# Transition matrices with time outermost, gathered per group by ScalarE, norms compacted by TensorE, and scales made between the query operations

## The chip, the cores and the metric

The kernel runs on one core of one Trainium2 chip. The metric is the device time of one launch in microseconds. 2335.91 us is the median of three runs of the kernel before (2333.31 to 2340.91).

## The reference

The layer is a recurrent mixer followed by a feed-forward block, on 8 rows of 512 time steps. Only the mixer is touched. For every head, with states `z` and `s` of N = 32 by DH = 16, it steps through time:

```
bc = (value @ W_bc.T).reshape(B, T, H, 4, N)
bc = bc / (sqrt(sum(bc*bc, axis=-1)) + EPS)          # Bz, Bx, Cz, Cx
S = 1 / (1 + dt*k + dt*dt*A)
z = S * (z - dt*A*s + dt*(Bz * u))
s = s + dt*z + dt*(Bx * u)
y = Cz . z + Cx . s
```

There are H = 32 heads. The scalars `dt` and `k` are of one head and time step, `A` is of one head and state.

## The kernel before

The program has three blocks: `project`, `mix` and `ffn`. `mix` works on 64 units, one for each row b (8) and group of four heads (8). A unit's 128 partitions are 4 heads by 32 states. Time is cut into NC = 8 chunks of C = 64 steps, all chunks computed in parallel, and only the states at the ends of chunks are passed on in order.

Each engine runs its own stream of instructions over the units, with semaphores between them. A loop over b runs seven times, its body unrolled over the 8 groups, and an eighth copy of the body stands behind it.

*TensorE* (`product`, `sum_squares`, `transpose_k`, `inner`, `outputs`): in a unit it transposes `k` (L716), makes three quarters of a product for the unit two ahead (L670), the states of the chunks `dX` (L704), the rest of that product, the scores (L695), two more products, in `outputs` a fourth one, the even inner outputs (L743), the sums of squares `ps_s` of the unit two ahead (L682: one matmul of 512 columns for each of the four vectors Bz, Bx, Cz, Cx), the outer outputs (L755) and the odd inner outputs (L743). Then it waits for the next `k`.

*ScalarE*: squares and copies each product (`evacuate`, L818 and L819), takes the root of the sums into `rows` (`norms`, L827), copies `kT`, `dX` and `y`, multiplies one row of the shear by A (`scale_beta`, L808), and makes the determinant `det` by a logarithm and an exponential (L858, L864).

*VectorE*: `body` scales the four vectors by the inverse norms (L1036, L1040), makes `k` (L1046 to L1060) and the queries `q` (L1065 to L1076), then `end` and `coef`, the scales of the next unit (`scales`: add epsilon, invert, multiply by the factors), the chain of states over the chunks (`V`, `cross`, `X`: L1098, L1103, L1109, seven times), the masked scores `g` (L1115) and a running sum for `det` (`log_sum`, L983). Between these, `advance(1)` puts one operation of `step_psi`: the 2 by 2 transition matrix of each chunk, `psi`, is stepped through its 64 time steps, for half of the groups (HALF = 4) at a time, four units ahead at least. A step is two operations on 128 partitions by 128 elements: `prod = psi * shear` (L958) and `psi = psi + prod` (L962), each waiting for the one before it. With 128 operations for a half and four units for it, 32 stand in a unit. `psi` is laid out as [row, component, group, chunk, time] and `shear` as [component, group, time], so time is the innermost axis and an operation of one time step takes every 65th element of `psi` and every 64th of `shear`.

*SyncE* issues the loads: the shear (`load_n_alpha`, `load_beta`), the norms' rows as a compact tile (`compact_norms`, four transfers for each unit between ScalarE's root and VectorE's scales), the scales to DRAM and back, spread over the partitions (`spread_scales`).

At the start, before the loop, the first half of row 0 is stepped alone (`step_rows`, L972 and L976, 256 operations of 128x64), with the first unit's scales in the middle.

## Time and profile before

| | |
|---|---|
| median of three runs | 2335.91 us |
| the profiled execution's own time | 2331.21 us |
| its span, first to last instruction | 2329.6 us |
| `mix` loop, unit 0 of row 0 to unit 0 of row 7 | 306.79 to 1812.81 us |
| VectorE busy, 1000 to 1500 us | 477.93 of 500 us |
| TensorE busy, 1000 to 1500 us | 428.09 of 500 us |
| ScalarE busy, 1000 to 1500 us | 238.69 of 500 us |
| granted TensorE clock, 1000 to 1500 us | 0.95 |

An engine is busy while one of its instructions runs. Matmuls overlap, and their ends are modelled. The granted clock is the share of full speed.

### The profile page before, as it was taken

What the parts mean: (1) busy time and instruction counts of PE and PEld (TensorE: products, weight loads), DVE (VectorE), ACT (ScalarE), POOL (GpSimd) and SP (SyncE); (2) the same over time, 40 slices, a digit from 0 to 9 for tenths busy, and PEclk for the clock granted to TensorE, in tenths of its full rate; (3) what the DMA queues carried; (4) which work ended last, traced back from release to release, by engine and by line L of the source; (5) the groups of instructions that cost most, each with busy time, mean ns of one, the idle gap of its engine ahead of it and who ended that gap; (6) DMA issues with size and microseconds to landing.
All of it is one profiled execution on the core that took longest, in us unless ns stands there. A gap on an engine that the chain in (4) does not pass through costs nothing. (4 is left out here: it accounts for less than half of the span.)

```text
span 2329.6 us, 78341 instructions
## 1 busy us (share of the span) xinstructions
PE 1875.7 (81%) x31266; PEld 1078.5 (46%) x31266; DVE 2050.5 (88%) x5467; ACT 1083.9 (47%) x1700; POOL 84.5 (4%) x28
## 2 busy tenths in 40 slices
PE   6777468987888898888888889887888898367886
PEld 3333134444444444444444444444444444246775
DVE  6887599999999999999989989998999998487774
ACT  4665235454444454445544444544545455034553
POOL 0000000000000000000000000000000000153300
PEclk9898779999999999999999999999999999578997
DMA  4555634655555565545655554665455543433400
GB/s 139 178 214 184 178 92 112 147 134 131 124 127 125 119 150 130 125 106 134 145 123 126 138 124 109 145 143 125 110 126 129 117 113 87 159 154 136 145 27 27
DMA packets 224663, 300.25 MB, mean 129 GB/s; under 512 B 96784, under 2 KB 114192, under 8 KB 218128
## 3 DMA queue, kind: packets, MB, share of 16 engines
q1 hardware_dynamic: 174416, 212.11, 35.9%
q10 hardware_dynamic: 48704, 78.68, 13.3%
q8 instruction: 252, 4.13, 0.8%
q0 software_dynamic: 1152, 4.19, 0.5%
q14 instruction: 139, 1.14, 0.2%
HBM read 240.85 MB, written 50.86 MB: 125 GB/s over the span
## 5 line engine op out<-in xcount | busy, mean ns | idle before, releaser
L670 PE MATMUL m_ps_a<-m_valT,m_w_bc 128*128 128x512 f32 x2048 | 962.1, 619 | 59.8 <-DMA m_valT<-scratch_valT 32.0
L670 PEld LDWEIGHTS m_ps_a<-m_valT,m_w_bc 128*128 128x128 f32 x2048 | 389.8, 198 | 491.1 <-issue 483.7
L958 DVE TENSOR_TENSOR m_prod<-m_psi,m_shear 128x128 f32<-128x128 f32 x960 | 369.0, 384 | 0.0
L962 DVE TENSOR_TENSOR m_psi<-m_psi,m_prod 128x128 f32<-128x128 f32 x960 | 368.4, 384 | 0.0
L818 ACT ACTIVATE m_sq<-m_ps_a 128x512 f32<-128x512 f32 x256 | 152.8, 597 | 372.4 <-PE m_ps_a L670 367.9
L833 ACT ACTIVATE m_kT<-m_ps_g 128x512 f32<-128x512 f32 x128 | 72.0, 596 | 249.8 <-PE m_ps_g L716 249.8
L716 PE MATMUL m_ps_g<-m_ident,m_k 128*128 128x128 f32 x512 | 88.9, 330 | 103.8 <-DVE m_k L1060 103.5
L695 PE MATMUL m_ps_g<-m_q,m_k 32*64 32x64 f32 x8192 | 122.8, 232 | 45.3 <-issue 38.9
L695 PEld LDWEIGHTS m_ps_g<-m_q,m_k 32*64 32x64 f32 x8192 | 107.5, 133 | 100.2 <-ACT m_dX L840 53.3
L819 ACT ACTIVATE m_raw<-m_ps_a 128x512 f32<-128x512 f32 x256 | 151.6, 592 | 0.0
L755 PEld LDWEIGHTS m_ps_y<-m_q,m_X 32*16 32x16 f32 x7168 | 105.2, 94 | 84.1 <-issue 84.1
L755 PE MATMUL m_ps_y<-m_q,m_X 32*16 32x64 f32 x7168 | 119.5, 218 | 28.9 <-issue 28.9
L221 PE MATMUL ps_w<-p_xnT,w_in 128*128 128x512 f32 x256 | 118.5, 617 | 14.6 <-ACT gate L284 14.6
L840 ACT ACTIVATE m_dX<-m_ps_g 128x128 f32<-128x128 f32 (+1 forms) x128 | 26.8, 261 | 221.5 <-PE m_ps_g L704 209.3
L716 PEld LDWEIGHTS m_ps_g<-m_ident,m_k 128*128 128x128 f32 x512 | 70.1, 168 | 115.9 <-DVE m_k L1060 113.8
L1036 DVE TENSOR_TENSOR m_raw<-m_raw,m_scale 128x1024 f32<-128x1024 f32 x64 | 77.5, 1210 | 49.7 <-issue 29.5
L743 PE MATMUL m_ps_y<-m_g,m_u 64*16 64x64 f32 x4096 | 89.8, 224 | 32.3 <-issue 25.4
L1267 POOL TENSOR_TENSOR f_y<-f_y,f_gate 128x2048 f32<-128x2048 f32 x8 | 38.4, 4805 | 1975.8 <-DMA f_svg<-scratch_svgT 1878.4
L743 PEld LDWEIGHTS m_ps_y<-m_g,m_u 64*16 64x16 f32 x4096 | 63.4, 95 | 89.5 <-issue 83.2
L827 ACT ACT_TABLE_LOAD x64 | 82.1, 1283 | 43.3 <-PE m_ps_s L682 43.2
L704 PEld LDWEIGHTS m_ps_g<-m_u,m_kT 64*32 64x32 f32 x7168 | 68.0, 106 | 63.9 <-issue 63.7
L1287 PE MATMUL f_ps_o<-f_w_out,f_y 128*128 128x256 f32 x256 | 61.6, 401 | 34.8 <-POOL f_y L1269 34.8
(143 smaller groups left out, 3061.7 us busy)
## 6 DMA issues: line engine op xcount, KB each, us to landing
m_scale<-scratch_norm SPq DMA_DIRECT2D x256, 256.0 KB, 5.3
m_w_bc<-in_w_bcT ACTq DMA_DIRECT2D x252, 256.0 KB, 4.7
m_shear<-scratch_n_alpha SPq DMA_DIRECT2D x64, 256.0 KB, 5.3
m_shear<-scratch_beta SPq DMA_DIRECT2D x256, 64.0 KB, 4.1
m_det<-scratch_gd SPq DMA_DIRECT2D x256, 64.0 KB, 4.5
scratch_gateT<-gate SPq DMA_DIRECT2D x8, 1024.0 KB, 3.9
scratch_valT<-val SPq DMA_DIRECT2D x8, 1024.0 KB, 4.5
scratch_svgT<-svg SPq DMA_DIRECT2D x8, 1024.0 KB, 5.5
```

The costliest lines, as they stand in the source:

```text
L221: mm = pe.matmul(ps_w[i % BANKS].ap(), w_in[:, k, col:col + P], xnT[:, k, :], start=(k == 0), stop=(k == KD - 1))
L670: mm = pe.matmul(ps_a[j % 2].ap(), w_bc[:, j, kt, :], valT[:, kt, :], start=(kt == 0), stop=(kt == KI - 1), skip_group_check=True)
L695: mm = pe.matmul(ps_g[rows_of(c), h, into], k[heads, part, cols], q[s][heads, part, cols], start=(part == 0), stop=(part == 1), skip_group ...
L716: mm = pe.transpose(ps_g[:, part, pair * P:(pair + 1) * P], k[:, part, pair * P:(pair + 1) * P], ident.ap())
L743: mm = pe.matmul(ps_y[h * N:h * N + DH, c * C:(c + 1) * C], u[rows_of(c), s, c // 2, h * DH:(h + 1) * DH], g[rows_of(c), h, c // 2 * C:(c ...
L755: pe.matmul(ps_y[h * N:h * N + DH, cols], X[heads, c - 1, part, :], q[s][heads, part, cols], start=False, stop=(part == 1), skip_group_che ...
L818: act.activation(sq[:, j, :], ps_a[j % 2].ap(), ACT.Square).then_inc(sq_ready.sem, sq_ready.step)
L819: act.activation(raw[s][:, j, :], ps_a[j % 2].ap(), ACT.Copy).then_inc(raw_ready.sem, raw_ready.step)
L827: act.activation(rows_.ap(), ps_s.ap(), ACT.Sqrt).then_inc(norm_ready.sem, norm_ready.step)
L958: dve.tensor_tensor(prod.ap(), psi_t[half][:, :, :, :, t], shear_t[half][:, :, :, t].unsqueeze(1).to_broadcast([P, 2, 2, HALF * NC]), ALU. ...
L962: ins = dve.tensor_tensor(psi_t[half][:, :, :, :, t + 1], psi_t[half][:, :, :, :, t], prod[:, :, ::-1, :], ALU.add)
L1036: dve.tensor_tensor(r4[:, 0:2, :], r4[:, 0:2, :], scale[:, 0:2, :], ALU.mult).then_inc(own.sem, own.one())
```

## The change

`psi` and `shear` get time as the outermost axis, so that the 128 elements of one time step lie together. The four groups of a half lie side by side in them. Since the operations on `k` and `q` need time innermost, ScalarE copies each unit's `psi` (2080 elements in a partition, read with a step of 128 elements) into a tile `psi_g` of the old form (`gather_psi`), and VectorE waits for it ahead of `k`. The shear is loaded into `stage` and laid out by two ScalarE copies with strided output for each group (`lay_shear`), instead of one in place.

`sum_squares` is cut into 8 segments of 64 columns. For each segment and vector a matmul with a selection matrix `seg_sum` puts the sums of head h and segment s into row h*8+s, so that the norms leave as a compact tile of 128x64, by 32 matmuls of 64 columns instead of 4 of 512. The root is taken straight into `compact`; the four transfers of `compact_norms` are gone.

The three operations of the scales stand between the queries' operations. `log_sum` stands ahead of `g`. `kt` uses the memory of `scale`, so SyncE loads the next scales after `q_ready`. The operations of `step_psi` are given to the four units as 36, 36, 36 and 20. At the start the shears of the first four groups are loaded into `raw`, and ScalarE lays them out by eight copies once all are there, before the first step; the gather of the first unit stands ahead of the evacuations of the second. `project` stores `beta` a second time, one more small transfer for each row.

```diff
+    SHARES = (0, 36, 72, 108, 2 * C)
...
-        psi = sb("psi", [P, 2, 2, HG, NC, C + 1])
-        shear = sb("shear", [P, 2, HG, T])
+        psi = sb("psi", [P, 2, C + 1, 2, 2, HALF * NC])
+        psi_g = sb("psi_g", [P, 2, 2, NC, C + 1])
+        shear = sb("shear", [P, 2, C, 2, HALF * NC])
+        stage = sb("stage", [P, 2, T])
         prod = sb("prod", [P, 2, 2, HALF * NC])
...
-        kt = sb("kt", [P, 2, T])
+        kt = scale[:, 0:2, :]
+        kT = sb("kT", [P, 2, T])
...
-                    sp.wait_ge(scaled.sem, scaled.at(b, group - 1))
+                    sp.wait_ge(q_ready.sem, q_ready.at(b, group - 1))
...
-                    for j in range(NJ):
-                        mm = pe.matmul(ps_s[j * N:(j + 1) * N, :], head_sum.ap(), sq[:, j, :],
-                                       start=True, stop=True, skip_group_check=True)
+                    for seg in range(SEGS):
+                        for j in range(NJ):
+                            mm = pe.matmul(ps_s[j * N:(j + 1) * N, 0:SEG], seg_sum[:, seg, :],
+                                           sq[:, j, seg * SEG:(seg + 1) * SEG],
+                                           start=(seg == 0), stop=(seg == SEGS - 1), skip_group_check=True)
...
-                def scale_beta(b, group):
-                    act.wait_ge(beta_in[group].sem, beta_in[group].at(b, HP - 1))
-                    act.activation(shear[:, 0, group, :], shear[:, 0, group, :], ACT.Copy,
-                                                  scale=A[:, group:group + 1]).then_inc(beta_scaled.sem, beta_scaled.step)
+                def lay_shear(b, group, src, loads=None):
+                    cols = slice(group % HALF * NC, (group % HALF + 1) * NC)
+                    dst = [shear[:, group // HALF, :, comp, cols].rearrange("p t c -> p c t") for comp in range(2)]
+                    act.wait_ge(shear_in.sem, shear_in.at(b, (loads or group + 1) * HP - 1))
+                    act.wait_ge(stepped.sem, stepped.at(b - 1, group // HALF))
+                    act.activation(dst[0], chunks(src[:, 0, :]), ACT.Copy, scale=A[:, group:group + 1])
+                    act.activation(dst[1], chunks(src[:, 1, :]), ACT.Copy).then_inc(shear_ready.sem, shear_ready.step)
+                def gather_psi(b, group):
+                    half, cols = group // HALF % 2, slice(group % HALF * NC, (group % HALF + 1) * NC)
+                    act.wait_ge(stepped.sem, stepped.at(b, group // HALF))
+                    act.wait_ge(raw_used.sem, raw_used.at(b, group - 1))
+                    act.wait_ge(coef_ready.sem, coef_ready.at(b, group - 1))
+                    act.activation(psi_g.ap().rearrange("p r k c t -> p (r k) c t"),
+                                   psi[:, half, :, :, :, cols].rearrange("p t r k c -> p (r k) c t"),
+                                   ACT.Copy).then_inc(psi_ready.sem, psi_ready.step)
...
-                    act.wait_ge(compact_in.sem, compact_in.at(b, group * NJ - 1))
-                    act.activation(rows_.ap(), ps_s.ap(), ACT.Sqrt).then_inc(norm_ready.sem, norm_ready.step)
+                    act.wait_ge(rows_stored.sem, rows_stored.at(b, group - 1))
+                    act.activation(compact.ap(), ps_s[:, 0:SEG], ACT.Sqrt).then_inc(norm_ready.sem, norm_ready.step)
...
+                        if more:
+                            gather_psi(b, group + 2)
                         if not last and group < LAST:
-                            scale_beta(b + 1, group + 1)
+                            lay_shear(b + 1, group + 1, stage)
...
-                            dve.tensor_tensor(prod.ap(), psi_t[half][:, :, :, :, t],
-                                              shear_t[half][:, :, :, t].unsqueeze(1).to_broadcast([P, 2, 2, HALF * NC]),
-                                              ALU.mult).then_inc(steps.sem, steps.one())
+                            dve.tensor_tensor(prod.ap().rearrange("p r k c -> p r (k c)"),
+                                              psi[:, half, t].rearrange("p r k c -> p r (k c)"),
+                                              shear[:, half, t].rearrange("p k c -> p (k c)").unsqueeze(1
+                                              ).to_broadcast([P, 2, 2 * HALF * NC]), ALU.mult).then_inc(steps.sem, steps.one())
                         else:
-                            ins = dve.tensor_tensor(psi_t[half][:, :, :, :, t + 1], psi_t[half][:, :, :, :, t],
+                            ins = dve.tensor_tensor(psi[:, half, t + 1], psi[:, half, t],
                                                     prod[:, :, ::-1, :], ALU.add)
...
+                def add_eps(b, group):
+                    dve.wait_ge(norm_ready.sem, norm_ready.at(b, group))
                     dve.tensor_scalar(compact.ap(), compact.ap(), NORM_EPS, None, ALU.add).then_inc(own.sem, own.one())
-                    between(1)
-                    dve.wait_ge(own.sem, own.n)
+                    return own.n
+                def invert_norms(eps_added):
+                    dve.wait_ge(own.sem, eps_added)
                     dve.reciprocal(compact.ap(), compact.ap()).then_inc(own.sem, own.one())
-                    between(1)
+                    return own.n
+                def apply_factors(b, group, inverted):
                     dve.wait_ge(factor_in.sem, factor_in.at(b, 3 * (group + 1) - 1))
-                    dve.wait_ge(own.sem, own.n)
+                    dve.wait_ge(own.sem, inverted)
                     dve.tensor_tensor(compact.ap(), compact.ap(), factor.ap(), ALU.mult).then_inc(rows_ready.sem, rows_ready.step)
...
+                        dve.wait_ge(psi_ready.sem, psi_ready.at(b, group))
...
+                        if here:
+                            eps_added = add_eps(b, group + 1)
+                        dve.tensor_tensor(by_chunk(q[s].ap())[:, ::-1], over_rows_of(r4[:, 3, :]),
+                                          psi_g[:, :, 0, :, 1:], ALU.mult).then_inc(raw_used.sem, raw_used.step)
                         cz_made = own.n
                         advance(1)
...
+                        if here:
+                            inverted = invert_norms(eps_added)
...
+                        if here:
+                            apply_factors(b, group + 1, inverted)
                         dve.tensor_tensor(q[s][:, 1, :], q[s][:, 1, :], kt[:, 0, :], ALU.subtract).then_inc(q_ready.sem, q_ready.step)
...
-                        if not (last and group == LAST):
-                            scales(b, group + 1, advance)
...
+                        if not (last and group == LAST):
+                            log_sum(b, group + 1)
```

TensorE, `outputs` of a unit: the even inner outputs (L743 before, L730 after), then the sums of squares of the unit two ahead. Before:

```order
L743 MATMUL m_ps_y<-m_g,m_u 16x64 [waits m_y_ready]
L743 MATMUL m_ps_y<-m_g,m_u 16x64 x15
L679 REGISTER_ALU
L680 REGISTER_ALU [waits m_sq_ready]
L682 MATMUL m_ps_s<-m_sq,m_head_sum 32x512 [waits m_norm_ready]
L682 MATMUL m_ps_s<-m_sq,m_head_sum 32x512 x3
```

After the change:

```order
L730 MATMUL m_ps_y<-m_g,m_u 16x64 [waits m_y_ready]
L730 MATMUL m_ps_y<-m_g,m_u 16x64 x15
L664 REGISTER_ALU
L665 REGISTER_ALU [waits m_sq_ready]
L668 MATMUL m_ps_s<-m_sq,m_seg_sum 32x64 [waits m_norm_ready]
L668 MATMUL m_ps_s<-m_sq,m_seg_sum 32x64 x31
```

The 4 matmuls of 512 columns are 32 of 64 columns; the profile counts two instructions and two weight loads for each, so 8 become 64. The waits and the neighbours are the same.

VectorE, from the second product of the queries (`m_q` on) towards the chain of states; `m_compact` is the tile of the scales. Before:

```order
L1068 TENSOR_TENSOR m_q<-m_raw,m_psi 128x2x512
L958 TENSOR_TENSOR m_prod<-m_psi,m_shear 128x128 [waits m_steps_dve]
L1074 TENSOR_TENSOR m_q<-m_kt,m_q 128x512 [waits m_raw_used,m_own_dve]
L962 TENSOR_TENSOR m_psi<-m_psi,m_prod 128x4x32 [waits m_steps_dve]
L1076 TENSOR_TENSOR m_q<-m_q,m_kt 128x512
L1080 TENSOR_TENSOR m_end<-m_det,m_e_end 128x16 [waits m_e_end_in]
L958 TENSOR_TENSOR m_prod<-m_psi,m_shear 128x128 [waits m_steps_dve]
L1085 TENSOR_TENSOR m_coef<-m_psi,m_end 128x32 [waits m_own_dve]
L962 TENSOR_TENSOR m_psi<-m_psi,m_prod 128x4x32 [waits m_steps_dve]
L997 ISA
L998 TENSOR_SCALAR m_compact<-m_compact 128x64 [waits m_compact_in]
L958 TENSOR_TENSOR m_prod<-m_psi,m_shear 128x128 [waits m_steps_dve]
```

After the change (`m_scale` is the tile that `kt` shares):

```order
L1076 TENSOR_TENSOR m_scale<-m_raw,m_psi_g 128x1024 [waits m_k_ready,m_own_dve]
L968 TENSOR_TENSOR m_psi<-m_psi,m_prod 128x128 [waits m_steps_dve]
L1002 REGISTER_ALU
L1003 TENSOR_SCALAR m_compact<-m_compact 128x64 [waits m_norm_ready]
L1081 TENSOR_TENSOR m_q<-m_raw,m_psi_g 128x2x512
L963 TENSOR_TENSOR m_prod<-m_psi,m_shear 128x128 [waits m_steps_dve]
L1008 RECIPROCAL m_compact<-m_compact 128x64 [waits m_own_dve]
L1089 TENSOR_TENSOR m_q<-m_scale,m_q 128x512 [waits m_raw_used,m_own_dve]
L968 TENSOR_TENSOR m_psi<-m_psi,m_prod 128x128 [waits m_steps_dve]
L1012 ISA
L1014 TENSOR_TENSOR m_compact<-m_compact,m_factor 128x64 [waits m_own_dve,m_factor_in]
L1093 TENSOR_TENSOR m_q<-m_q,m_scale 128x512
```

The scales' three operations (the first stands last but one in the listing of before, its two followers behind it) move up from behind `coef` to between the queries' operations, and the first waits for ScalarE's root instead of a transfer.

ScalarE, from the logarithm of a unit (`m_det`) to the next evacuation of a product (`m_sq`, `m_raw`). Before:

```order
L858 ACT_TABLE_LOAD
L858 ACTIVATE m_det<-m_det,m_one,m_nA 128x512 [waits m_gd_in1]
L808 ACTIVATE m_shear<-m_shear,m_A 128x512 [waits m_beta_in2]
L816 REGISTER_ALU
L818 ACTIVATE m_sq<-m_ps_a 128x512 [waits m_sums_made,m_a_made]
L819 ACTIVATE m_raw<-m_ps_a 128x512
L821 DMA m_w_bc<-in_w_bcT 128x512
```

After the change:

```order
L859 ACT_TABLE_LOAD
L859 ACTIVATE m_det<-m_det,m_one,m_nA 128x512 [waits m_gd_in1]
L808 ACTIVATE m_psi_g<-m_psi 128x2080 [waits m_coef_ready,m_raw_used,m_stepped]
L797 ISA
L799 ACTIVATE m_shear<-m_stage,m_A 128x8x64 [waits m_stepped,m_shear_in]
L800 ACTIVATE m_shear<-m_stage 128x8x64
L817 REGISTER_ALU
L819 ACTIVATE m_sq<-m_ps_a 128x512 [waits m_sums_made,m_a_made]
L820 ACTIVATE m_raw<-m_ps_a 128x512
L822 DMA m_w_bc<-in_w_bcT 128x512
```

The gather, with three waits, and a second copy for the shear now stand between the logarithm and the evacuation that TensorE's products wait for.

## Rows read from the trace of the kernel before

**Rows 1.** The page: busy time, share of span and instructions of each engine.
```profile
PE 1875.7 (81%) x31266; PEld 1078.5 (46%) x31266; DVE 2050.5 (88%) x5467; ACT 1083.9 (47%) x1700; POOL 84.5 (4%) x28
```

**Rows 2.** Timeline of VectorE, first operation of units: start, duration, [idle before, releaser].
```profile
306.79 1.21 DVE L1036 TENSOR_TENSOR m_raw<-m_raw,m_scale 128x1024 f32<-128x1024 f32 x1
...
1035.52 1.23 DVE L1036 TENSOR_TENSOR m_raw<-m_raw,m_scale 128x1024 f32<-128x1024 f32 x1
...
1061.13 1.20 DVE L1036 TENSOR_TENSOR m_raw<-m_raw,m_scale 128x1024 f32<-128x1024 f32 x1
...
1386.26 1.22 DVE L1036 TENSOR_TENSOR m_raw<-m_raw,m_scale 128x1024 f32<-128x1024 f32 x1 [4.75 <-issue]
...
1812.81 1.22 DVE L1036 TENSOR_TENSOR m_raw<-m_raw,m_scale 128x1024 f32<-128x1024 f32 x1 [1.87 <-DMA m_scale<-scratch_norm]
```

**Rows 3.** Waits of all engines, 300 to 1900 us: us in total, times, longest.
```profile
PE m_ps_g L716 <- DVE m_k L1060: 98.0, 47, 6.7
...
PE m_ps_g L695 <- issue: 35.9, 42, 1.4
...
PE m_ps_y L755 <- issue: 28.9, 16, 3.7
...
PE m_ps_y L743 <- issue: 24.5, 15, 3.2
```

**Rows 4.** Timeline of TensorE in the last row of the batch.
```profile
1948.78 1.09 PE L716 MATMUL m_ps_g<-m_ident,m_k 128*128 128x128 f32 x8
...
1966.79 0.64 PE L743 MATMUL m_ps_y<-m_g,m_u 64*16 64x64 f32 x32
1967.54 1.06 PE L682 MATMUL m_ps_s<-m_sq,m_head_sum 128*32 128x512 f32 x8
1968.54 1.75 PE L755 MATMUL m_ps_y<-m_q,m_X 32*16 32x64 f32 x112
...
1970.79 1.09 PE L716 MATMUL m_ps_g<-m_ident,m_k 128*128 128x128 f32 x8
```

**Rows 5.** Two stretches, the first behind a wait for `k`: us, TensorE busy (instructions), granted clock, DMA share, GB/s.
```profile
1232.00:1238.00 6.00, 5.81 (x27) 0.62 0.10 21
...
1948.00:1970.00 22.00, 21.78 (x477) 1.00 0.36 78
```

**Rows 6.** VectorE by line and shape, 300 to 1900 us: busy, mean ns, idle before.
```profile
L962 DVE TENSOR_TENSOR m_psi<-m_psi,m_prod 128x128 f32<-128x128 f32 x946 | 363.0, 384 | 0.0
L1103 DVE TENSOR_TENSOR m_cross<-m_coef,m_V 128x64 f32<-128x64 f32 x354 | 76.5, 216 | 0.0
...
L1074 DVE TENSOR_TENSOR m_q<-m_kt,m_q 128x512 f32<-128x512 f32 x59 | 40.5, 686 | 0.0
```

**Rows 7.** Timeline of VectorE in the chain of states of one unit.
```profile
1057.00 0.38 DVE L958 TENSOR_TENSOR m_prod<-m_psi,m_shear 128x128 f32<-128x128 f32 x1
1057.30 0.18 DVE L1109 TENSOR_TENSOR m_X<-m_cross 128x32 f32<-128x32 f32 x1
1057.42 0.40 DVE L962 TENSOR_TENSOR m_psi<-m_psi,m_prod 128x128 f32<-128x128 f32 x1
```

**Rows 8.** ScalarE by line and shape, 300 to 1900 us, then 200 to 300 us.
```profile
L808 ACT ACTIVATE m_shear<-m_shear,m_A 128x512 f32<-128x512 f32 x56 | 38.9, 707 | 0.0
L864 ACT ACTIVATE m_det<-m_det 128x512 f32<-128x512 f32 x60 | 37.9, 631 | 30.8 <-DVE m_det L983 30.3
...
L277 ACT ACTIVATE ek<-p_compact 128x128 f32<-128x128 f32 x1 | 0.3, 292 | 0.0
```

**Rows 9.** Timeline of ScalarE behind the logarithm of one unit.
```profile
1272.12 0.60 ACT L818 ACTIVATE m_sq<-m_ps_a 128x512 f32<-128x512 f32 x1 [2.75 <-PE m_ps_a L670]
...
1275.55 0.60 ACT L818 ACTIVATE m_sq<-m_ps_a 128x512 f32<-128x512 f32 x1 [2.35 <-PE m_ps_a L670]
```

**Rows 10.** VectorE by line and shape, 225 to 306 us, where row 0 starts.
```profile
L976 DVE TENSOR_TENSOR m_psi<-m_psi,m_prod 128x64 f32<-128x64 f32 x128 | 28.8, 276 | 0.0
...
L998 DVE TENSOR_SCALAR m_compact<-m_compact 128x64 f32<-128x64 f32 x1 | 0.2, 196 | 6.2 <-DMA m_compact<-m_rows 6.2
```

137 lines of the change are left out of this document (59 added, 78 removed).

## The prediction

> **What bounds the kernel now.** I read the page first: VectorE is busy for 88% of the span, TensorE for 81%, ScalarE for 47% [rows 1]. Then the timeline of VectorE at the first operation of each unit. In the loop a unit with no wait takes 1061.13 - 1035.52 = 25.6 us on VectorE [rows 2], back to back. Seven rows of the batch take 1812.81 - 306.79 = 1506.0 us [rows 2], 215.1 us for each row of 8 units. That is 8 x 25.6 = 204.8 us and 10.3 us of waits; about half of these is the start of a loop turn, where VectorE stands for 4.75 us with nothing that releases it ("issue") [rows 2].
>
> VectorE is the bound, but not by far. TensorE waits for `k` 98.0 us in 1600 us, 59 units, which is 1.7 us a unit [rows 3]. In the last row of the batch no steps are made, so VectorE is light there, and TensorE shows its own length: from one unit's transposes to the next 1970.79 - 1948.78 = 22.0 us [rows 4], with the full work and almost no gap. In ordinary units it also stands inside its bursts of small matmuls, again on "issue": 35.9 + 28.9 + 24.5 = 89.3 us in those 59 units [rows 3], 1.5 us each. So TensorE's own length is 22.0 + 1.5 = 23.5 us against VectorE's 25.6, and what VectorE saves beyond 2.1 us in such a unit is not to be had.
>
> **The steps on VectorE.** The 32 step operations of a unit take 384 ns each at 128x128 [rows 6]. Two neighbours with contiguous operands give the line for contiguous ones: 216 ns at 64 elements and 686 ns at 512 [rows 6], 1.05 ns an element, 283 ns at 128. The difference, 100 ns, is what taking every 64th or 65th element costs, 0.78 ns for each. The chain of dependences doesn't hide it: the operation after a step starts 0.30 us behind it, the next step 0.12 us later, when the first (0.38 us) has just ended [rows 7]; a step of 0.28 us lets both move up by 0.10 us. Bounds: nothing, if the stride isn't the reason, and 0.17 us, if the step came down to the 216 ns of half the elements. I take 0.10, since both operands become contiguous: 32 x 0.10 = 3.2 us, so 22.4 us a unit. In the units with 36 operations four stand in a row at the end, where each waits out the one ahead (0.28 and a few hundredths instead of 0.20): 3 x 4 x 0.12 us in four units, some 0.4 each, so 22.8 us.
>
> The Trainium skill ("SBUF — State Buffer", section "SBUF: two separate sides") says that SBUF is read in lines of 16 bytes and that an access which crosses to a new line each time pays a penalty. The trace agrees, with 384 against 283 ns; the page gives no figure. The same rule speaks against the change on ScalarE, which now does the strided walk.
>
> **The gather and the lays on ScalarE.** No row has ScalarE jump through memory. Contiguous copies from SBUF take 292 ns at 128 and 631 ns at 512 elements [rows 8], 0.88 ns each, so 2080 elements take 2.0 us at least. With VectorE's extra of 0.78 ns on each it is 3.6 us. As the far end I take four times the contiguous price, 7.4 us. I take 3.6, since the walk is of the same kind (a new place for each element). The two lays, 512 elements each with a strided output, are 0.63 + 0.40 = 1.0 us each by the same extra, in place of one of 0.71 [rows 8]. Together 3.6 + 2.0 - 0.7 = 4.9 us more, all of it between the logarithm and the next evacuation. Queued behind it is that evacuation, which frees the buffer of TensorE's fourth product. There ScalarE waits 2.75 us for TensorE now, and at the next product 2.35 us more [rows 9]: TensorE makes that product, 1275.55 - 1272.12 = 3.4 us, in the other buffer before it needs this one, and the evacuation itself takes 3.4 - 2.35 = 1.1, so 2.3 us of delay pass unseen. The room is 2.75 + 2.3 = 5.0 us, and 4.9 just fit. The gather's own waits don't count: `coef` is made on VectorE before the chain of states starts, while ScalarE still copies `dX`; in the two units of eight where the last steps stand in the chain of states, they end in its middle. On the other side, VectorE needs `psi_g` only after the chain of states, `g` and two multiplies of the next unit; its wait there would hold `k` and with it TensorE's transposes.
>
> **The norms on TensorE.** The sums take 1968.54 - 1967.54 = 1.0 us now [rows 4]. After, they are 64 instructions of 64 columns on 32 output rows. The nearest row is the even inner outputs, 32 instructions of 64 columns that go to four column groups in turn as these do: 0.64 us, 20 ns each [rows 4]. 64 x 20 = 1.25 us, 0.25 more. From below: no more than now, since as many columns pass. From above: the transposes, 8 with 128 columns of weights and 128 moving, 1.09 us [rows 4], which is 136 ns each or 0.53 ns a column; 96 columns for each of the 64 would be 51 ns, 3.3 us, 2.3 more.
>
> The Trainium skill ("TensorE: Matmul & The Clock Gate", section "Part 3: Packing small matmuls — row/col tiling") says that a weight load overlaps with running matmuls only when the row group differs; here all four vectors use all rows. By it the dear end would hold. The even inner outputs all stand on the same rows too and go at 20 ns, so the trace speaks against it.
>
> TensorE has to be fed 56 more matmuls and as many weight loads in each unit, 64 x 56 = 3584 beside the program's 31266 [rows 1], all inside a burst. I let the "issue" gaps grow from 1.5 to 1.9 us; bounds are the 1.5 of now and 2.8 (a gap of a microsecond more for the second half of a burst that is twice as long).
>
> **The scales and the transfers.** The removed transfers cost VectorE little in the loop, where nothing but the loop's start and single late scales (1.87 us once [rows 2]) holds up a unit. I cost them at nothing. The root is taken before ScalarE copies `kT`, so the first operation of the scales finds it there. SyncE now waits for the lay of the group ahead before it loads a shear; the scales behind that in its queue are due half a unit later. They are loaded after `q_ready`, under the chain of states (20 pairs as in rows 7, 20 x 0.32 = 6.4 us), `log_sum` and `g`; without that cover they would come late as in rows 2, by 2 us or more. `log_sum` ahead of `g` makes `g` 1.2 us later, covered by the products that TensorE makes between scores and outputs.
>
> **The start.** Before row 0's loop VectorE waits 6.2 us for the compact norms [rows 10]; that goes. The 256 operations of 128x64 at 276 ns [rows 10] come to 216 [rows 6], but every one has a neighbour to overlap, so about 0.04 us each, 10 us in all. Against it: eight lays of 1.0 us, which begin when all loads are there, put off the first step by some 6 us, and the first gather (3.6 us) stands ahead of the second unit's evacuations. Together -6 us.
>
> **The sum.** VectorE 22.8 us, TensorE 22.0 + 0.25 + 1.9 = 24.15 us: TensorE is the bound. As each waits for the other within a unit (`k`, `dX`, the scores), I add 0.15: 24.3 us. The start of a loop turn stays, 5 us. A row is 8 x 24.3 + 5 = 199.4 us, 15.7 less than 215.1. Seven rows: -110. The last row: four units at 24.3, -6, and the rest, bound by TensorE already, +1. The start: -6. Together -121: the profiled execution's own 2331.2 us becomes 2210. The median of the runs is 4.7 us above that execution, so 2215. The granted clock enters through the 22.0 us, a row at the upper level: a stretch behind a wait for `k` shows 0.62, this unit 1.00 [rows 5], and with TensorE as the bound such waits are left at loop starts alone.
>
> **Rivals.**
> *More gaps in TensorE's feed.* With 2.8 us a unit is 25.2 us, a row 206.6: 7 x -8.5, -2 and -6 give 2263 and a median of 2268. For it: TensorE no longer pauses for `k`, in which time it could be fed. Against: the unit of 22.0 us had the same bursts and no gap.
> *No gaps.* Then TensorE needs 22.25 us and VectorE's 22.8 bind; with 0.5 for waits between the two (VectorE's chain of states can't start before TensorE's `dX`), a unit is 23.3 us, a row 191.4: 7 x -23.7, -9 and -6 give 2150, median 2155.
> *The weight loads of the sums don't overlap.* The unit is 22.0 + 2.3 + 1.9 + 0.15 = 26.35 us, a row 215.8, no gain; with the start 2330, median 2335.
> *The gather is dear.* This one ends slower. Beyond the room of 5.0 us each microsecond goes to TensorE's fourth product, so to the unit. The gain of 2.0 us a unit is gone from a gather of about 5.7 us on, 2.8 times the contiguous price. At 7.4 us the unit is 24.3 + 3.7 = 28.0 us, a row 229: 2331 + 7.5 x 14 - 6 = 2430. For it: no row shows ScalarE's price of jumping, and its steps here are 512 bytes. Against: VectorE pays 1.75 times for such steps.
> *The steps don't get shorter*, as their price isn't the stride's: VectorE stays at 25.6 and pays for the four in a row (0.42 us each for 0.30), 26.0 us and 0.3 of waits, a row 215.4: with ScalarE's load and the start about 2345.
>
> **How the numbers follow.** Chances: the forecast 0.60, with a range of its own of 2185 to 2250; more gaps 0.13; no gaps 0.07; weight loads 0.07; a dear gather 0.10; steps no shorter 0.03. From 2150 to 2300 the first three hold, 0.80. A measurement of this kernel can tell about 0.3%, 7 us. Faster: the first three and a part of the weight loads, 0.82; within 0.3%: most of the rest of the weight loads, 0.03; slower 0.15.
>
> **What would show it.** The steps at about 284 ns, and no idle time of VectorE but at loop starts and ahead of `X` and `g`. `gather_psi` at 3.6 us and the lays at 1.0. The sums' 64 matmuls within 1.3 us. TensorE's wait for `k` near zero, its "issue" rows grown to 110 us or so, a row of the batch at 199 us. The forecast is wrong if ScalarE ends a gather so late that TensorE's fourth product waits for `raw`, or if the sums take over 2 us.

## The result, and the profile after

The changed kernel takes 2463.09 us (median of four runs, 2445.14 to 2468.45) against 2336.97 us before, a ratio of 1.0526 [1.0468, 1.0584]. The forecast was 2215 us, the range 2150 to 2300. So it is slower by 5%, on the side of the rivals, and by none of them.

The page first. TensorE and VectorE are both busy for less of a longer span than in [rows 1]: neither engine is full, so something stands between them. The line on queue q8 is that of instruction transfers (packets, MB, share).

```profile
PE 1939.9 (79%) x34850; PEld 1153.1 (47%) x34850; DVE 1885.5 (76%) x5472; ACT 1379.8 (56%) x1828; POOL 83.1 (3%) x28
...
q8 instruction: 277, 4.54, 0.8%
```

The operations that the prediction priced, by line and shape, 300 to 1900 us (busy, mean ns, idle before), answer to [rows 6, 8] and to the sums in [rows 4]:

```profile
L968 DVE TENSOR_TENSOR m_psi<-m_psi,m_prod 128x128 f32<-128x128 f32 x883 | 253.5, 287 | 2.8
...
L808 ACT ACTIVATE m_psi_g<-m_psi 128x2080 f32<-128x2080 f32 x56 | 213.4, 3810 | 1.5 <-DVE m_psi L968 1.3
...
L799 ACT ACTIVATE m_shear<-m_stage,m_A 128x512 f32<-128x512 f32 x55 | 65.1, 1183 | 0.0
...
L668 PE MATMUL m_ps_s<-m_sq,m_seg_sum 128*32 128x64 f32 x3520 | 61.5, 222 | 11.3 <-ACT m_sq L819 5.7
...
L800 ACT ACTIVATE m_shear<-m_stage 128x512 f32<-128x512 f32 x55 | 60.3, 1097 | 0.0
```

All are near what was priced: steps 287 ns (284), gather 3.81 us (3.6), lays 1.18 and 1.10 (1.0 each), sums 61.5 / 55 = 1.12 us a unit (1.25). The loss is not in them. It shows in the waits of the same stretch, against [rows 3]:

```profile
DVE m_cross L1118 <- ACT m_dX L841: 186.4, 53, 7.7
ACT m_dX L841 <- PE m_ps_g L691: 173.9, 55, 4.6
...
PE m_ps_g L682 <- issue: 137.2, 41, 4.9
DVE m_raw L1067 <- ACT m_det L865: 87.9, 35, 5.6
...
PE m_ps_y L742 <- issue: 48.1, 28, 3.5
...
PE m_ps_y L730 <- issue: 17.0, 13, 1.6
PE m_ps_g L691 <- issue: 16.6, 14, 1.9
...
PE m_ps_g L703 <- DVE m_k L1071: 10.7, 6, 2.3
```

The wait for `k` is nearly gone (10.7 us, 98.0 before), but TensorE now stands 137.2 us inside the scores (L682), in gaps of up to 4.9 us that end in "issue", where before it stood 35.9 us with none over 1.4. VectorE's two long waits are for ScalarE: for `dX`, for which ScalarE itself waits for TensorE, and for `det`. The second falls to 1.2 us in thin_scales below, so it is a consequence and not a cause.

VectorE's first operation of the first, fifth and last row of the batch gives the rows' length, as [rows 2] does: (1930.51 - 306.71) / 7 = 232.0 us for 8 units, against 215.1 before and 199.4 forecast.

```profile
306.71 1.23 DVE L1045 TENSOR_TENSOR m_raw<-m_raw,m_scale 128x1024 f32<-128x1024 f32 x1 [2.68 <-DMA m_scale<-scratch_norm]
...
1227.28 1.23 DVE L1045 TENSOR_TENSOR m_raw<-m_raw,m_scale 128x1024 f32<-128x1024 f32 x1 [3.67 <-ACT m_raw L820]
...
1930.51 1.23 DVE L1045 TENSOR_TENSOR m_raw<-m_raw,m_scale 128x1024 f32<-128x1024 f32 x1 [1.83 <-DMA m_scale<-scratch_norm]
```

Two units on TensorE's timeline, the first without a gap and the second with one (start, duration, [idle before, releaser]):

```profile
1001.96 1.09 PE L703 MATMUL m_ps_g<-m_ident,m_k 128*128 128x128 f32 x8 [2.04 <-DVE m_k L1071]
...
1007.75 1.70 PE L682 MATMUL m_ps_g<-m_q,m_k 32*64 32x64 f32 x128
...
1120.21 1.09 PE L703 MATMUL m_ps_g<-m_ident,m_k 128*128 128x128 f32 x8
...
1125.92 1.10 PE L682 MATMUL m_ps_g<-m_q,m_k 32*64 32x64 f32 x75
1130.45 0.87 PE L682 MATMUL m_ps_g<-m_q,m_k 32*64 32x64 f32 x53 [3.43 <-issue]
1131.25 12.22 PE L655 MATMUL m_ps_a<-m_valT,m_w_bc 128*128 128x512 f32 x24
```

And SyncE's timeline at the same places, the issue of the next unit's scales (four loads of 256 KB):

```profile
1008.08 2.64 SPq L594 DMA_DIRECT2D m_scale<-scratch_norm  x4
...
1123.01 1.76 SPq L594 DMA_DIRECT2D m_scale<-scratch_norm  x4
```

In the first unit the load is issued 6.1 us behind the start of the transposes, and the scores go through in 1.70 us. In the second it is issued 2.8 us behind, and the scores are cut in two by 3.43 us. Windows of the second unit (length, then busy time and instructions of TensorE, its weight loads, VectorE, ScalarE and GpSimd, then granted clock, DMA share, GB/s) show the rest:

```profile
1124.00:1128.00 4.00, 3.02 (x189) 2.10 (x172) 2.42 (x15) 2.37 (x5) 0.00 (x0) 1.00 0.92 249
1128.00:1132.00 4.00, 1.54 (x54) 1.23 (x55) 4.00 (x26) 3.99 (x3) 0.00 (x0) 0.90 0.96 206
1132.00:1136.00 4.00, 4.00 (x7) 1.58 (x6) 3.86 (x11) 2.92 (x3) 0.00 (x0) 0.67 0.03 10
```

The DMA engines are full (0.92, 0.96) just while TensorE goes through small matmuls, and after the gap its granted clock reads 0.67, between its two levels (0.5 and 1.0 of full speed), and the 24 products take 12.22 us (10.59 us for the same 24 in thin_scales, below, behind a gap of 1.24). I took the distance from the transposes' start to the load's issue ("lag") for all units from these two timelines: of 55 units in 300 to 1900 us, 36 have a lag under 5 us, with 3.6 us of gap in the scores on average and 30.1 us from transposes to transposes; 19 have 5.5 us or more, with 0.5 us of gap and 26.9 us. Before, the median lag was 9.1 us and the smallest 6.8.

This comparison flatters the lag, and so do the two units above, for the place in the program counts too. In the seven rows of the loop the gap in a fifth unit always stands behind the 75th of the 128 instructions of the scores (as in the second unit above), in the changed kernel as in hold and thin_scales below. The first and the last unit of a row have no such place: in none of the three do their scores have a gap that ends in "issue". The first unit above is one of these, and so are 13 of the 19. Units at the same place of the row compare fairly: in the second unit, loads 6.2 us or more behind the transposes leave 0 to 1.3 us of gap, and loads under 5 us behind them 3.1 to 3.7 us; in the third, 5.5 us already gives 2.7. So the gap does grow as the load comes closer. It is not the lag alone that counts, since the fifth units of hold_states (below) have 0.6 to 1.2 us of gap at a lag of 4.8; which distance does was not tried by itself.

### The profile page after: what moved, and what is told of

Read it like the earlier page. It is cut to its first block and busy times, and to the rows that moved or that the text cites. A ratio compares the mean times of both kernels' runs of the same rounds, so it can differ in the third digit from the quotient of the medians.

```text
span 2466.8 us, 85589 instructions
## 1 busy us (share of the span) xinstructions
PE 1939.9 (79%) x34850; PEld 1153.1 (47%) x34850; DVE 1885.5 (76%) x5472; ACT 1379.8 (56%) x1828; POOL 83.1 (3%) x28
## 3 DMA queue, kind: packets, MB, share of 16 engines
q8 instruction: 277, 4.54, 0.8%
## 5 line engine op out<-in xcount | busy, mean ns | idle before, releaser
L655 PE MATMUL m_ps_a<-m_valT,m_w_bc 128*128 128x512 f32 x2048 | 1015.7, 647 | 78.4 <-ACT m_raw L820 38.4
L655 PEld LDWEIGHTS m_ps_a<-m_valT,m_w_bc 128*128 128x128 f32 x2048 | 407.3, 208 | 545.2 <-issue 513.1
L963 DVE TENSOR_TENSOR m_prod<-m_psi,m_shear 128x128 f32<-128x128 f32 x960 | 275.2, 287 | 5.8 <-ACT m_shear L800 1.9
L968 DVE TENSOR_TENSOR m_psi<-m_psi,m_prod 128x128 f32<-128x128 f32 x960 | 275.6, 287 | 3.1
L682 PE MATMUL m_ps_g<-m_q,m_k 32*64 32x64 f32 x8192 | 137.3, 254 | 158.3 <-issue 154.5
L808 ACT ACTIVATE m_psi_g<-m_psi 128x2080 f32<-128x2080 f32 x64 | 243.8, 3809 | 1.5 <-DVE m_psi L968 1.3
L682 PEld LDWEIGHTS m_ps_g<-m_q,m_k 32*64 32x64 f32 x8192 | 120.2, 151 | 214.5 <-issue 162.5
L1118 DVE TENSOR_TENSOR m_cross<-m_coef,m_dX 128x64 f32<-128x64 f32 x64 | 14.4, 225 | 210.1 <-ACT m_dX L841 209.9
L742 PE MATMUL m_ps_y<-m_q,m_X 32*16 32x64 f32 x7168 | 125.8, 222 | 52.5 <-issue 52.5
L1067 DVE TENSOR_TENSOR m_raw<-m_raw,m_det 128x1024 f32<-128x1024 f32 x64 | 78.2, 1222 | 109.1 <-ACT m_det L865 109.0
L730 PE MATMUL m_ps_y<-m_g,m_u 64*16 64x64 f32 x4096 | 90.2, 224 | 27.1 <-issue 20.8
L730 PEld LDWEIGHTS m_ps_y<-m_g,m_u 64*16 64x16 f32 x4096 | 63.9, 96 | 85.1 <-issue 79.1
```

The lines of the kernel that those rows point to most:

```text
L655: mm = pe.matmul(ps_a[j % 2].ap(), w_bc[:, j, kt, :], valT[:, kt, :], start=(kt == 0), stop=(kt == KI - 1), skip_group_check=True)
L682: mm = pe.matmul(ps_g[rows_of(c), h, into], k[heads, part, cols], q[s][heads, part, cols], start=(part == 0), stop=(part == 1), skip_group ...
L730: mm = pe.matmul(ps_y[h * N:h * N + DH, c * C:(c + 1) * C], u[rows_of(c), s, c // 2, h * DH:(h + 1) * DH], g[rows_of(c), h, c // 2 * C:(c ...
L742: pe.matmul(ps_y[h * N:h * N + DH, cols], X[heads, c - 1, part, :], q[s][heads, part, cols], start=False, stop=(part == 1), skip_group_che ...
L808: act.activation(psi_g.ap().rearrange("p r k c t -> p (r k) c t"), psi[:, half, :, :, :, cols].rearrange("p t r k c -> p (r k) c t"), ACT. ...
L963: dve.tensor_tensor(prod.ap().rearrange("p r k c -> p r (k c)"), psi[:, half, t].rearrange("p r k c -> p r (k c)"), shear[:, half, t].rear ...
```

## The experiments

**Theory A**: the 1 MB load of the scales, which now comes earlier, runs into TensorE's small matmuls and delays its supply of instructions. **B**: ScalarE's added 5 us a unit hold the evacuations back. **C**: the 56 more instructions of the sums outrun the supply by themselves. The table has every run; ratios are to the kernel before in the same call (medians 2342 to 2356 us, for the changed kernel 2337). Gaps are TensorE's idle time on "issue" in 300 to 1900 us; the lag is the median.

| run | us | ratio | in the scores | in the outputs | lag |
|---|---|---|---|---|---|
| before | 2337 | 1 | 35.9 | 53.4 | 9.1 |
| changed | 2463 | 1.0526 [1.0468, 1.0584] | 137.2 | 65.1 | 3.2 |
| hold | 2362 | 1.0092 [1.0059, 1.0125] | 33.5 | 92.0 | 9.5 |
| half_gather | 2454 | 1.0478 [1.0415, 1.0542] | 132.0 | 64.1 | 3.0 |
| psi_only | 2365 | 1.0084 [1.0050, 1.0118] | 47.7 | 42.7 | 7.4 |
| early_scales | 2376 | 1.0135 [1.0101, 1.0169] | 46.3 | 24.2 | 6.8 |
| thin_scales | 2295 | 0.9779 [0.9746, 0.9812] | 50.7 | 74.5 | 5.0 |
| hold_sums | 2385 | 1.0137 [1.0096, 1.0178] | 36.7 | 12.2 | 8.6 |
| hold_order | 2393 | 1.0184 [1.0150, 1.0217] | 29.9 | 16.6 | 8.5 |
| hold_both | 2393 | 1.0202 [1.0166, 1.0238] | 36.5 | 10.9 | 8.7 |
| hold_long_sums | 2273 | 0.9692 [0.9653, 0.9731] | 36.2 | 35.5 | 8.6 |
| hold_states | 2308 | 0.9841 [0.9799, 0.9883] | 37.8 | 74.7 | 6.2 |
| hold_half_gather | 2359 | 1.0052 [1.0029, 1.0076] | 30.9 | 107.9 | 10.0 |
| long_sums | 2275 | 0.9686 [0.9610, 0.9762] | 58.5 | 27.7 | 6.3 |
| hold_wide | 2287 | 0.9791 [0.9740, 0.9842] | 37.9 | 47.6 | 9.0 |
| more_sums | 2358 | 1.0084 [1.0053, 1.0116] | 35.3 | 80.8 | 8.7 |
| slow_pe | 2300 | 0.9814 [0.9790, 0.9838] | 42.4 | 0 | 4.9 |
| slow_pe_held | 2284 | 0.9742 [0.9720, 0.9765] | 36.4 | 0 | 5.0 |
| wide | 2298 | 0.9811 [0.9751, 0.9870] | 39.8 | 46.3 | 7.7 |
| slower_pe | 2519 | 1.0709 [1.0672, 1.0746] | 60.9 | 0 | 4.2 |

**1. hold.** The load waits for the scores:

```diff
                     sp.wait_ge(q_ready.sem, q_ready.at(b, group - 1))
+                    sp.wait_ge(g_made.sem, g_made.at(b, group - 1))
```

> The changed kernel, with the load of the next unit's scales held until the unit's scores are multiplied. Theory A (the 1 MB load runs into TensorE's bursts of small matmuls and delays its instruction fetch, and the gaps cost the rest): the gaps that end in "issue" ahead of the scores fall from 140 us in the stretch 300 to 2000 to 40 us or less, a unit from about 29 us to 24 to 25.5, and the time to 2230 us (2200 to 2300). Theory B (ScalarE's 3.8 us gather and 1.1 us lays hold the evacuations back): the time stays over 2420 us, with the waits for the determinant's inverse as long as now. Theory C (the 64 small matmuls of the sums of squares, in the place of 4, shift the fetch): the gaps ahead of the scores stay near 140 us and the time near 2460.

The gaps in the scores fell to 33.5 us, as A said, and 101 us came off; B and C said 2420 and more. But 2362 us is not the 2230 that A gave: the gaps in the outputs grew from 65.1 to 92.0 us. The DMA engines are busier during the outputs there (share 0.45, 0.20 in the changed kernel, medians over the units of the traces), but that this makes the larger gaps is not shown. The hold also puts off the loads that stand behind the scales in SyncE's queue (`u`, the factors, `gd`), so this run alone doesn't say which bytes count.

**2. half_gather.**

```diff
-                    act.activation(psi_g.ap().rearrange("p r k c t -> p (r k) c t"),
-                                   psi[:, half, :, :, :, cols].rearrange("p t r k c -> p (r k) c t"),
+                    act.activation(psi_g[:, 0], psi[:, half, :, 0, :, cols].rearrange("p t k c -> p k c t"),
...
```

> The changed kernel with ScalarE's gather of half of the states' columns left out (one of the two rows; the output is not the reference's). The gather takes about 1.9 us instead of 3.8. Theory A: ScalarE's work is not the bound, the gaps ahead of the scores stay near 140 us in the stretch 300 to 2000, and the time stays over 2420 us. Theory B: 1.9 us a unit come off a chain that sets the time, 64 units give 120 us or more, and the time falls to about 2340 us or less. Theory C: as A.

The gather took 1.99 us, and the time hardly moved: 2454 us (three runs, 2442 to 2472; a fourth, the one in the trace, took 2484), where B gave 2340 or less. B falls.

**3. psi_only.** The changed states, gather and lays; head sums, compact transfers and the scales' place as before.

> The changed kernel's states, gather and lays, with the norms, their transfers, the place of the scales' operations and of the log's sum as in the kernel before. The scales are then ready later, and the 1 MB load starts later. Theory A: gaps ahead of the scores near 36 to 60 us in the stretch 300 to 2000, and a time of 2230 to 2330 us. Theory B: the gather and the lays alone make the loss: over 2400 us. Theory C: the sums of squares are 4 long matmuls again, so the gaps are gone here too: 2230 to 2330 us, which is not told from A by this run alone, but by the next one.

2365 us, over the range. B said 2400 or more. VectorE waits 85.7 us for the compact norms and 58.1 us for the scales here, against 4.0 and 8.4 before: with a faster VectorE the old chain of transfers seems too long. One unit of the row loses its scores here too, without any short sums; slower_pe below comes back to it.

**4. early_scales.** The kernel before, with the scales' three operations between the queries':

```diff
...
+                        if here:
+                            eps_added = add_eps(b, group + 1)
                         dve.tensor_tensor(by_chunk(q[s])[:, ::-1], over_rows_of(r4[:, 3, :]),
...
```

> The kernel before, with the scales' three operations alone moved between the queries' operations, so that the 1 MB load starts earlier. Theory A: the gaps ahead of the scores grow from 36 us in the stretch 300 to 2000 to 60 us or more, and the time to 2350 to 2400 us, unless VectorE reaches these operations so late that the load still comes after the scores. Theories B and C: neither ScalarE's work nor the sums have changed, so the time stays at 2337 us, within 10.

The lag fell from 9.1 to 6.8 us only, presumably since VectorE was no faster; the time rose by 1.35%, within what A gave for the time, but the gaps in the scores grew only to 46.3 us, not to 60.

**5. thin_scales.** The early load with 1/16 of its bytes:

```diff
-                        sp.dma_start(scale[h * N:(h + 1) * N, :, :], spread(src)).then_inc(
+                        sp.dma_start(scale[h * N:(h + 1) * N, :, 0:32], spread(src[:, 0:32])).then_inc(
...
```

> The changed kernel without the hold; of the scales' load only 32 of 512 columns are moved (1/16 of the bytes, at the same place in the program; the rest of the scales is left out, so the output is not the reference's). Theory A (bytes in flight in TensorE's bursts): the gaps ahead of the scores fall from 140 us in the stretch 300 to 2000 to 40 us or less although the load is released as early as in the changed kernel, and the time falls to the level of the held load (2362 us) or lower, since nothing waits for the scales: 2230 to 2365 us. Rival A2 (it is not the bytes but the order in SyncE's queue and the early release itself): the gaps stay over 100 us and the time over 2420 us.

168 us came off. The gaps in the scores are 50.7 us, over the 40 that A gave, but none is longer than 1.8 us:

```profile
PE m_ps_y L742 <- issue: 55.6, 29, 4.0
PE m_ps_g L682 <- issue: 50.7, 45, 1.8
```

A fifth unit of a row, with the load issued at 1055.48 us, 2.6 us behind its transposes, and the gap behind the same 75th instruction:

```profile
1052.84 1.09 PE L703 MATMUL m_ps_g<-m_ident,m_k 128*128 128x128 f32 x8
...
1058.56 1.10 PE L682 MATMUL m_ps_g<-m_q,m_k 32*64 32x64 f32 x75
1060.89 0.87 PE L682 MATMUL m_ps_g<-m_q,m_k 32*64 32x64 f32 x53 [1.24 <-issue]
```

Twenty-one units still have a lag under 4 us, and their gap is 1.2 us. So it is the bytes in flight, not the early release. The gaps of 1 us stay. The DMA engines aren't idle then: their share around these gaps, from 1.5 us ahead of a gap to its end, is 0.51 (median), against 1.0 in the changed kernel. The gaps in the outputs (74.5 us, up to 4.0) stay as well, so the bytes of the scales don't make most of those.

**6. hold_sums, hold_order, hold_both.** On top of hold: the sums of two vectors moved between long products; the gather put behind the second evacuation; both.

> The held load (2362 us), and half of the sums of squares (the first two of four vectors) moved out of the burst of outputs to between long products. Theory C2 (what is left of the loss is that the longer burst outruns its instruction fetch): the gaps within and ahead of the outer outputs and the inner outputs, 98 us in the stretch 300 to 2000 with the held load, fall to 60 us or less, and the time to 2310 to 2345 us. Theory A alone (only transfers in flight make the gaps): the gaps there change by less than 15 us, and the time stays at 2362 us, within 12.

> The held load, and ScalarE's gather and lay behind the evacuation of TensorE's second product instead of ahead of it. Theory B2 (what is left is ScalarE's added 5 us that put off that evacuation): TensorE's waits for the evacuation, 20 us beside the one at the start in the stretch 300 to 2000, go, ScalarE is late at the third instead, and the time falls by 15 to 25 us to 2340. Rival: the delay only moves on to the next evacuation, or TensorE would stand anyway, and the time stays at 2362, within 12.

> The held load with both edits, the sums moved and the gather behind the second evacuation. If C2 and B2 both hold: 2290 to 2325 us, faster than the kernel before. If neither: 2362 us, within 12.

All three are slower than hold. In hold_sums the gaps in the outputs went (92.0 to 12.2 us), but the sums of one vector, one after the other on the same output rows, cost TensorE four times as much (61.5 us for 55 units in the changed kernel):

```profile
L665 PE MATMUL m_ps_s<-m_sq,m_seg_sum 128*32 128x64 f32 x3712 | 230.4, 222 | 9.3 <-ACT m_sq L835 3.3
```

In hold_order the delay only moves: TensorE's sums now wait 143.7 us for the last squares, and the gaps in the outputs fell (92.0 to 16.6 us). hold_both has the cost of the first. None of them decides on C2 or B2.

**7. hold_long_sums.** As many columns in 4 matmuls instead of 32:

```diff
-                    for seg in range(SEGS):
-                        for j in range(NJ):
-                            mm = pe.matmul(ps_s[j * N:(j + 1) * N, 0:SEG], seg_sum[:, seg, :],
-                                           sq[:, j, seg * SEG:(seg + 1) * SEG], ...
+                    for j in range(NJ):
+                        mm = pe.matmul(ps_s[j * N:(j + 1) * N, :], seg_sum[:, 0, :], sq[:, j, :], ...
```

> The held load (2362 us), with the sums of squares as 4 matmuls of 512 columns again in the place of 32 of 64 columns: as much time on TensorE (1.06 us for 1.10), 56 instructions and as many weight loads fewer in the burst of outputs. The sums come out wrong by this, so the output is not the reference's. Theory C2 (the longer burst outruns its instruction fetch): the gaps in the outputs, 98 us in the stretch 300 to 2000 with the held load, fall to the 54 us of the kernel before, and the time falls by 30 to 60 us, to 2300 to 2335 us. Theory A alone (transfers in flight make all that is left): gaps change by less than 15 us, the time stays at 2362 us, within 12.

89 us came off hold's 2362, more than C2 gave; the outputs' gaps fell to 35.5 us.

**8. hold_states.** As hold, with `dX_made` in the place of `g_made`.

> The load of the scales held until the products for the states are done, 2.5 us or so ahead of the end of the scores where hold waits. With the held load the transfer shows in the DMA share only 2 to 3 us behind its issue, so by theory A most of it still lies behind the scores, the gaps ahead of them stay at 40 to 60 us in the stretch 300 to 2000, the end of the transfers moves away from the outputs, whose gaps fall from 98 to 75 us or less, VectorE waits less than 46 us for the scales, and the time is 2330 to 2355 us. Rival (any part of it in the scores starves them): the gaps ahead of the scores go over 90 us and the time to 2390 us or more.

2308 us: better than A gave (2330 to 2355), and 1.6% faster than the kernel before, with nothing left out. With a lag of 6.2 us the scores are as clear as with hold (37.8 us), and the DMA share during the outputs is back at 0.22.

**9. hold_half_gather.**

> The held load with half of ScalarE's gather left out (one of two rows, so the output is not the reference's). Theory B2 (with the collision gone, ScalarE's added work counts): TensorE's waits for an evacuation, 20 us in the stretch 300 to 2000 beside the one at the start, go, and with the slack that VectorE and TensorE get the time falls by 15 to 40 us to 2322 to 2347. Theory A alone: 2362 us, within 12.

2359 us. B2 falls too: ScalarE's work isn't what is left.

**10. long_sums, hold_wide, more_sums.** Long sums without a hold; hold_states with 16 sums of 128 columns (`SEG` doubled, four stores); the kernel before with the 64 short sums added.

> The changed kernel without any hold, with the sums of squares as 4 matmuls of 512 columns (the sums come out wrong by this, so the output is not the reference's). It completes the square of early or held load and short or long sums: 2463 us (early, short), 2362 (held, short), 2273 (held, long). If the two losses add up, the short sums cost 89 us here too: 2374 us, with the gaps ahead of the scores still over 110 us in the stretch 300 to 2000. If the early load only starves TensorE because the longer burst has used up what was fetched ahead: 2273 to 2310 us, with gaps ahead of the scores below 60 us. If the early load hurts more once the sums are short in instructions (VectorE bound no more): over 2400.

> The load held until the products for the states are done (2308 us), and the sums of squares by 16 matmuls of 128 columns in the place of 32 of 64: the norms leave TensorE on 64 partitions of 128 columns, stored by four transfers in the place of one; the output is the reference's. 24 of the 56 extra instructions of a unit stay, as many columns pass. If the count of instructions is what costs: half or more of the 90 us that long sums gave come back, 2245 to 2280 us. If the gain of the long sums came from something else (their wrong values, fewer stops on output rows): 2300 to 2325 us, VectorE's 0.8 us more a unit among it.

> The kernel before, with the 64 instructions of 64 columns put in ahead of its own sums of squares, which then overwrite them; all else as before, the load of the scales too. TensorE's own time grows by 1.1 us a unit, most of it hidden where it waits for k (1.7 us a unit). Theory C2 (instructions alone cost gaps): the gaps on issue in the stretch 300 to 2000 grow from 108 us to 140 or more, and the time to 2375 to 2430 us. If the count alone does little without the early load: gaps below 125 us, 2347 to 2375 us.

long_sums decided: 2275 us, as good as with the hold. The square of early or held load and short or long sums, with the same hold in both, reads 2463, 2362, 2275, 2273: the early load costs 101 us with short sums and nothing with long ones. But its lag is 6.3 us, twice that of the changed kernel, though the release is the same. The start of its unit behind the one from 1043.94 us shows why:

```profile
1068.78 1.09 PE L701 MATMUL m_ps_g<-m_ident,m_k 128*128 128x128 f32 x8 [0.97 <-DVE m_k L1069]
```

TensorE waits for `k` again, so VectorE is not ahead, and its load comes later against TensorE's bursts. hold_wide came 21 us under hold_states, with 0.5 us a unit more on VectorE and four stores: it lies between its two ranges, 7 us over what the count of instructions was to give. (The 89 us are a difference to hold; from hold_states to the long sums it is 35.) more_sums shows the short sums by themselves on the kernel before: 0.8%, as "the count alone does little" had it. The gaps in the outputs grew (53.4 to 80.8 us), those in the scores did not.

**11. slow_pe, slow_pe_held, wide, slower_pe.** To see whether the early load needs the short sums: the long sums, with TensorE made slower by two (slow_pe) or five (slower_pe) long products, and the wide sums with no hold.

```diff
+                    for _ in range(2):
+                        pe.matmul(ps_s.ap(), ident.ap(), sq[:, 3, :], start=True, stop=True, skip_group_check=True)
                     for j in range(NJ):
```

> The changed kernel with the long sums (2275 us; sums wrong, so the output is not the reference's) and two added products of 512 columns ahead of them, whose result is overwritten: 1.76 us a unit more for TensorE, in long matmuls that need hardly any fetch. The load of the scales is released by q_ready as in the changed kernel. Theory F (feedback: whatever makes TensorE the slower engine lets VectorE, and with it the load, run ahead into TensorE's own bursts): the load is issued about 3 us behind the start of the transposes instead of 6 to 7, the gaps ahead of the scores grow from 58 us to 110 or more in the stretch 300 to 1900, and the time exceeds 2275 by more than all of the added work (64 x 1.76 = 113): over 2390 us. Rival (the starved bursts need the short sums' extra instructions): the gaps stay under 75 us and the time is 2340 to 2388 us.

> The same with the load held until the products for the states are done. Theory F: the gaps ahead of the scores stay under 60 us in the stretch 300 to 1900, and the time is 2330 to 2375 us, 50 us or more under the one without the hold. Rival: the two are within 15 us of each other.

> The sums by 16 matmuls of 128 columns with the load not held (held: 2287 us; the output is the reference's). Between short (held or not, 2308 and 2463) and long sums (2273 and 2275). Theory F: with 24 instead of 56 extra instructions TensorE and VectorE are about equal, the load is issued 5 to 7 us behind the transposes, and the time is 2270 to 2310 us. Rival: already 24 extra instructions let the load run ahead: over 2350 us, with gaps ahead of the scores of 80 us or more in the stretch 300 to 1900.

> As slow_pe, with five added products instead of two (sums wrong as there): TensorE's own length grows by 2.6 to 2.8 us a unit more, so the next unit's load, which follows VectorE, comes as early against TensorE as in the changed kernel: about 3 us behind the start of the transposes (slow_pe 4.9, changed 3.2, long_sums 6.3). Theory F2 (an early load alone starves the scores, the short sums are needed only to make TensorE slow): the gaps ahead of the scores grow from 42 to 110 us or more in the stretch 300 to 1900, and the time exceeds 2300 + 64 x 2.7 = 2473 us by 50 or more: over 2520 us. Theory C3 (it takes the short sums' instructions; without them the early load costs little): gaps ahead of the scores under 60 us, and 2440 to 2490 us.

slow_pe missed both ranges: 2300 us, only 25 more for 2.0 us of added work a unit (122.5 us for 61 units), while the gaps in the outputs (27.7 us) and TensorE's waits for `k` (28.9 us) went. Its lag is 4.9 us, and its gaps in the scores are small (42.4 us); the hold gains 17 us, near the rival's 15 and far from F's 50. wide, at 2298 us, is within F's time, with a lag of 7.7 us (F gave 5 to 7) and gaps as small as in hold_wide. slower_pe's time lies between the two ranges and says nothing, as a wait of its own came in (VectorE waits 151.1 us for the norms); its gaps in the scores, 60.9 us, are far under the 110 of F2. But three of its units have a lag of 3.3 us, and they stand 3.6, 4.1 and 4.4 us in their scores, without the short sums of squares in the program. One of them on TensorE's timeline, with the load issued at 1426.38 us:

```profile
1423.10 1.09 PE L703 MATMUL m_ps_g<-m_ident,m_k 128*128 128x128 f32 x8 [0.60 <-issue]
...
1429.78 1.66 PE L682 MATMUL m_ps_g<-m_q,m_k 32*64 32x64 f32 x125
1435.58 0.33 PE L682 MATMUL m_ps_g<-m_q,m_k 32*64 32x64 f32 x3 [4.14 <-issue]
```

At 4.0 to 4.4 us most of its gaps are 0.7 to 2.4 us. psi_only shows the same more often, with the four long sums of the kernel before: in the seventh unit of its rows the gap stands behind the 107th instruction of the scores, as it does in the kernel before, but it is 2.0 to 4.1 us at lags of 3.8 to 5.9 us, where the kernel before has 0.3 to 1.1 us at lags of 6.8 to 8.8. One of them, with the load issued at 1157.02 us:

```profile
1152.90 1.97 PE L713 MATMUL m_ps_g<-m_ident,m_k 128*128 128x128 f32 x8
...
1160.38 1.49 PE L692 MATMUL m_ps_g<-m_q,m_k 32*64 32x64 f32 x107
1165.93 0.52 PE L692 MATMUL m_ps_g<-m_q,m_k 32*64 32x64 f32 x21 [4.06 <-issue]
```

So an early load starves the scores without the short sums, in the units that have such a place in their scores; the short sums are one way to bring it that early. The lag doesn't tell all: the fifth units of more_sums have lags of 3.0 to 4.2 us and no gap in the scores.

**The late packet.** The trace keeps every packet of the instruction queue q8. For each gap over 0.5 us in the scores, 300 to 1900 us, I took the last such packet and compared its times with the gap's (medians):

```
kernel        gaps   packet starts, against gap's start   gap ends, behind packet's end
before          40   1.62 us ahead                        1.37 us
changed         41   0.75 us behind                       1.52 us
thin_scales     43   1.22 us ahead                        1.42 us
hold_states     42   1.67 us ahead                        1.45 us
```

In every kernel the gap ends about 1.5 us after a packet has landed (nine in ten within 1.2 to 1.7 us). In the other three, where the DMA share around these gaps is 0.35 to 0.58, the packet sets out before TensorE runs dry, and the gap is about 1 us; in the changed kernel, at a share of 1.0, it sets out some 2.4 us later, when TensorE is dry already. This is the middle link of theory A. That the packet waits behind the scales' packets on the same DMA engines is inferred: from the DMA share in the windows, and from its coming in time again when the bytes are taken away.

The Trainium skill ("Runtime: NRT & Kernel Launch", section "Instruction fetch mechanics") says that instructions are fetched in blocks of 16 KiB by a DMA queue of the sequencer's own, and that crossing into a new block is mostly hidden. The size agrees (4.54 MB in 277 packets); hidden it is not in these bursts, where gaps of up to 1.4 us stay in the scores with the load held as well. That the gaps keep their places in the program fits such blocks.

## Why the prediction was wrong

**The step that failed** is in the paragraph on the scales and the transfers. It costs the removed transfers at nothing, and the load that is moved has no term in the sum at all. Of it the paragraph asked only whether VectorE would get its scales in time (the cover under the chain of states, which held: VectorE waits 2.7 us for them in 55 units). It did not ask whom 1 MB in flight disturbs when it comes 6 us earlier against TensorE's work. The runs put a size on it: without the bytes 168 us less, with the load held to the end of the states 155 us less, with it held to the end of the scores 101 us less, of the 248 us between forecast and result.

**Why it came so early.** The forecast saw that TensorE would become the bound and stopped there. VectorE, waiting for TensorE at the chain of states, then does the next unit's queries and releases the load a nearly fixed time after that. Lag and unit together make 3.2 + 29.1 = 32.3 us in the changed kernel, 6.3 + 25.8 = 32.1 in long_sums and 4.9 + 26.2 = 31.1 in slow_pe (units as 1600 us by their number). Within the changed kernel's trace, too, a long unit goes with a short lag in the next one (correlation -0.75 over 55 units). So the longer TensorE's unit, the earlier the load falls in the next one; the gap makes the unit longer, and so keeps the load early. This is argued from these sums, not shown by a run of its own, and slower_pe, with 4.2 + 29.6 = 33.8 us, fits less well. The units of a row go the same way: the first of the row that starts at 994.2 us, behind a loop turn, takes 24.2 us by VectorE's first operations, the later ones 26.2 to 34.4.

**The gaps in TensorE's feed** were forecast to grow from 1.5 to 1.9 us a unit by the 56 instructions. In the outputs and the products for the states that was right: (28.9 + 24.5 + 11.3) / 60 = 1.1 us before, (48.1 + 17.0 + 16.6) / 55 = 1.5 after. In the scores they went from 35.9 / 60 = 0.6 to 137.2 / 55 = 2.5 us, most of it by the load (50.7 / 61 = 0.8 without its bytes). With 10.2 / 55 = 0.2 us ahead of the products of L655 the gaps come to 4.2 us. The rival "more gaps" had the right engine, but 2.8 us for gaps of 4.2, since it reckoned with longer bursts only.

**TensorE's own 22.25 us** rested on the upper clock level throughout. Behind a gap the granted clock reads 0.67, and TensorE is busy for 1325.33 us in those 1600, 24.1 us a unit. So 24.1 + 4.2 + 0.8 (waits for evacuations, 24 of the 43.3 us at one place) + 0.2 (for `k`) = 29.3 us, near the 1600 / 55 = 29.1 measured; the forecast was 24.3 and 5 us a row.

**What was right**: the steps, the gather, the lays, the sums, ScalarE's room (the rival "dear gather", which ended on the measured side, falls by half_gather and hold_half_gather), and TensorE as the bound. (The two rows of ScalarE that the prediction calls copies are exponentials, of 292 and 631 ns; its prices from them came out near all the same.) The unit of 24.3 us exists: the first units of the changed kernel's rows, whose scores have no gap, take 23.9 to 24.4 us by VectorE's first operations in six rows of seven, and long_sums has 24.0 us in its undisturbed units. A row there takes (1759.80 - 310.06) / 7 = 207.1 us, 7.7 more than forecast, from a few units of 27 to 32 us in each row; whose transfers lengthen these was not tried. The start brought nothing (306.71 us before row 0's loop, 306.79 before), where I had 6 us.

**What stays open**: what part of the 89 us of the long sums on the held load is instructions and what is a collision that ends sooner. And 80 us or more stand between the forecast and both thin_scales and hold_states; the gaps in the outputs (74.5 and 74.7 us in 1600) are part of them, and what makes those is not shown. hold_wide, the best version that leaves nothing out, takes 2287 us.

## What to carry to other kernels

When a change makes an engine faster, ask not only what its transfers wait for, but into which stretch of the other engines they will now fall: bursts of small matmuls live on instruction packets, and here these came late where a large load kept the DMA engines full. To see it, look whether a gap stands at the same instruction each time. Where the lag of a transfer is set by an engine that runs ahead, tie its release to the engine that it can disturb (here one wait, `dX_made`: 2463 to 2308 us). And count instructions beside columns: the same columns in 32 short matmuls or 4 long ones take the same 1.1 us, and still differ by 89 us with the load held and by 188 us with it early.

## What the runs showed of the hardware

A stop of TensorE in a burst ended about 1.5 us after an instruction packet had landed, with the DMA engines full (share 1.0) and half full (0.35 to 0.58) alike, and in the scores it stood at the same instruction of the program in each row of the loop. Sixteen sums on the same output rows in a row take as long (1.08 us) as 64 that go through the four groups of rows in turn (1.10 us). ScalarE's copy with a step of 512 bytes between elements took 3.81 us for 2080 elements and 1.99 us for 1040, so 1.75 ns for each further element, against 0.88 ns by the two contiguous exponentials of [rows 8].
